# Sigmoid cross-attention: the last key's contribution moved from PE's output product to a POOL term that DVE's extraction starts from

## The reference, cut to what matters

```python
def _L1_xattn_ref(query, key, value, Wq, Wk, Wv, Wo):
    H, D, scale = 16, 16, 16 ** (-0.5)
    q = (query @ Wq.T).reshape(B, L, H, D) * scale
    k = (key @ Wk.T).reshape(B, -1, H, D)
    v = (value @ Wv.T).reshape(B, -1, H, D)
    scores = jax.nn.sigmoid(jnp.einsum('blhd,bshd->bhls', q, k))
    o = jnp.einsum('bhls,bshd->blhd', scores, v).reshape(B, L, E)
    return o @ Wo.T

x = x + _L1_xattn_ref(_layernorm(x, axis=-1), ctx_1024, ctx_1024, ...)   # x: [128, 32, 256], ctx_1024: [128, 257, 256]
```

## Time and profile before

| | |
|---|---|
| runs, us | 3064.57, 3067.11, 3067.53 |
| median of the runs, us | 3067.11 |
| the profiled execution's own time, us | 3058.71 |
| its span (first to last instruction), us | 3056.9 |
| mean clock granted to PE, of 2.4 GHz | 0.926 |
| PE busy over the span | 2633.2 us (86%), 31182 matmuls |
| DVE, ACT, POOL busy over the span | 66%, 59%, 54% |
| this layer | 1594 to 2294 us of the span |
| PE, DVE, ACT, POOL busy in these 700 us | 665, 509, 472 and 418 us |

### The profile page before, as it was taken

One profiled execution on the slowest core, in us unless ns is written; L12 is line 12 of the kernel. 1 busy time (PEld: TensorE's weight loads), 2 busy tenths in 40 slices (PEclk: granted clock), 3 DMA queues, 4 the chain that ended last, 5 costly groups with the idle time before them and its releaser, 6 DMA issues. The chain is left out here.

```text
span 3056.9 us, 81164 instructions
## 1 busy us (share of the span) xinstructions
PE 2633.2 (86%) x31182; PEld 2052.3 (67%) x31182; DVE 2019.7 (66%) x4510; ACT 1814.4 (59%) x4252; POOL 1652.4 (54%) x1589
## 2 busy tenths in 40 slices
PE   2999999999985988986797999999994888527998
PEld 2888888888863655553355888888873666416776
DVE  4677777777764777776346777777766888653443
ACT  2667767667666777772345777777763666343333
POOL 3666666666635777773006666666644777142332
PEclk9999999999996999887798999999996999558999
DMA  5333332223300000000002212221200000451110
GB/s 145 85 84 85 84 82 76 75 77 84 92 28 1 1 1 1 1 1 14 16 15 84 64 49 64 64 64 49 64 18 16 2 2 2 170 181 48 38 40 26
DMA packets 120951, 160.04 MB, mean 52 GB/s; under 512 B 11456, under 2 KB 107840, under 8 KB 118400
## 3 DMA queue, kind: packets, MB, share of 16 engines
q1 hardware_dynamic: 115904, 140.28, 16.1%
q0 software_dynamic: 4672, 14.57, 1.3%
HBM read 139.99 MB, written 14.83 MB: 51 GB/s over the span
## 5 line engine op out<-in xcount | busy, mean ns | idle before, releaser
L570 ACT ACTIVATE x_prob<-x_prob,x_nm 128x257 f32<-128x257 f32 x512 | 254.5, 499 | 212.7 <-DVE x_nm L656 212.7
L1894 DVE TENSOR_TENSOR_SCAN m_s<-m_a,m_psD 128x1024 f32<-128x1024 f32 x128 | 284.9, 2267 | 3.0 <-PE m_psD L1721 2.9
L656 DVE CUSTOM_DVE_ANT_0 x_prob<-x_psS,x_masked,x_lastv 128x256 f32<-128x256 f32 x512 | 217.3, 481 | 104.0 <-PE x_psS L476 100.7
L1195 DVE SCALAR_TENSOR_TENSOR x_pTl<-x_psS,x_pTh 128x1024 f16<-128x1024 f32 x128 | 156.7, 1225 | 144.9 <-ACT x_pTh L1103 144.9
L1833 ACT ACTIVATE m_a<-m_dt,m_rate 128x248 f32<-128x248 f32 x512 | 206.9, 493 | 0.0
L2778 ACT ACTIVATE e1t_g<-e1t_psH,e1t_bias 128x128 f32<-128x128 f32 x312 | 89.2, 368 | 171.1 <-PE e1t_psH L2727 171.1
L1605 POOL TENSOR_TENSOR m_s<-m_s 128x1024 f32<-128x1024 f32 x64 | 150.6, 2354 | 68.5 <-DVE m_s L1894 68.5
L883 POOL TENSOR_TENSOR x_qbdh<-x_qh,all_mask4h 128x1024 f16<-128x1024 f16 x32 | 60.6, 1894 | 215.8 <-DVE x_ql L1176 215.8
L1116 ACT ACTIVATE x_vh<-x_psV 128x512 f16<-128x512 f32 x128 | 76.4, 597 | 134.4 <-PE x_psV L922 134.4
L875 POOL TENSOR_TENSOR x_ctxl<-x_ctx,x_ctxh 128x512 f16<-128x512 f32 x128 | 149.7, 1170 | 10.7
L318 POOL TENSOR_TENSOR x_ctxl<-x_ctx,x_ctxh 128x512 f16<-128x512 f32 x128 | 148.3, 1159 | 10.7
(11 more groups left out here) (591 smaller groups left out, 10617.9 us busy)
## 6 DMA issues: line engine op xcount, KB each, us to landing
x_ctx<-in_ctxT SPq DMA_DIRECT2D x64, 1024.0 KB, 6.2
x_mraw<-in_mask SPq DMA_DIRECT2D x128, 128.5 KB, 6.0
x_vxr<-x_vx SPq DMA_DIRECT2D x32, 512.0 KB, 6.9
e1r_stage<-in_L_ffn_w SPq DMA_DIRECT2D x16, 1024.0 KB, 5.0
e_rows<-e1r_pad POOLq DMA_DIRECT2D x1, 5070.0 KB, 19.6
e1t_row<-e_rows SPq DMA_DIRECT2D x39, 130.0 KB, 2.1
all_xres<-in_x SPq DMA_DIRECT2D x1, 4096.0 KB, 14.4
x_vxr<-x_vx SPq DMA_DIRECT2D x128, 32.0 KB, 3.5
```

The lines of the kernel that those rows point to most:

```text
L570: last = act.activation(prob[b % NP][:, s, :], prob[b % NP][:, s, :], ACT.Exp, bias=nm[b % NP][:, s:s + 1], scale=-1.0, accum_out=sm[b // ...
L656: dve.tensor_tensor_reduce(prob[b % NP][:, s, 0:LAST], psS[:, s * LAST:(s + 1) * LAST], masked[g % 2][:, j, :], -SC, lastv[g % 2][:, j, s: ...
L1195: dve.scalar_tensor_tensor(pT[c % 4][1][:].rearrange("p r k n -> p (r k n)"), psS[c % 2][:], PS, pT[c % 4][0][:].rearrange("p r k n -> p ( ...
L1894: dve.tensor_tensor_scan(states, rates, psD[at % 2][:], 0.0, ALU.mult, ALU.add).then_inc(scan_done, 1)
```

## The change

The last key's term no longer goes through psO. `last_scores` multiplies by a 128x128 matrix `same_head` that is 1 where two channels belong to the same head, so that the score of a head comes out on each of its 16 channels, for both halves of the channels (two matmuls into 256 columns of psM instead of two that add up in 64 rows). ACT makes one sigmoid of it (128x256, f32). The last key's values are made with channels on partitions and kept in SBUF in f32 (`vx`). POOL's `last_term` multiplies the two into `term` (128x256, f32) in the place of `own_rows`. DVE's extraction makes all four passes, the first with `term` as what is added to; ACT's pass goes. The two matmuls at the end of `attend`, the f16 copies and low parts of the last probabilities, the writes to DRAM and the four row loads of each group go.

```diff
-        (vxp,) = parts("vx", [P, D], 1)
-        vxr = [sb(f"vxr{n}", [64, GB, D], F16) for n in range(2)]
-        vxm = [sb(f"vxm{n}", [64, GB, D], F16) for n in range(2)]
-        own_head, head_sum = sb("own_head", [64, D], F16), sb("head_sum", [P, C, 64], F32)
+        vx = sb("vx", [P, NT, C, GB], F32)
+        same_head = sb("same_head", [P, P], F32)
...
-        px32 = sb("px32", [64, P], F32)
-        px3 = [sb(f"px3_{n}", [64, P], F16) for n in range(2)]
+        px = [sb(f"px{n}", [P, C * P], F32) for n in range(2)]
+        term = [sb(f"term{n}", [P, C, GB, T], F32) for n in range(2)]
...
-        psA, psX = psM[:, 0:256], psM[0:64, 256:384]
+        psA, psX = psM[:, 0:256], psM[:, 256:512]
...
-            sync.dma_start(own_head[:], d["x1_own_head"]).then_inc(const_in, 16)
-            sync.dma_start(head_sum[:], d["x1_head_sum"]).then_inc(const_in, 16)
+            sync.dma_start(same_head[:], d["x1_same_head"]).then_inc(const_in, 16)
...
-            def load_vx(i, gp):
-                g = i * 2 + gp
-                wait_apart(sync, vxm_ready, g - 1, sync_passed)
-                for r in range(4):
-                    src = vx_dram[r % 2:r % 2 + 1, bass.ds(g * GB, GB), :].to_broadcast([16, GB, D])
-                    sync.dma_start(vxr[gp][16 * r:16 * r + 16], src).then_inc(vxr_in[gp], 16)
-
             load(0, 0)
             load(0, 1)
-            sync.wait_ge(vx_lo, 1)
-            for k in range(2):
-                sync.dma_start(vx_dram[k], vxp[k][:]).then_inc(vx_out, 16)
-            sync.wait_ge(vx_out, 32)
 
             def body(i):
                 for gp in range(2):
                     if not (isinstance(i, int) and i == 0):
                         load(i, gp)
-                    load_vx(i, gp)
...
-            def own_rows(i, gp):
+            def last_term(i, gp):
                 g = i * 2 + gp
-                wait_apart(pool, vxr_in[gp], (i + 1) * 64, pool_passed)
-                wait_apart(pool, pv_mm, (g - 1) * GB, pool_passed)
-                pool.tensor_tensor(vxm[gp][:], vxr[gp][:], own_head[:].unsqueeze(1).to_broadcast([64, GB, D]), ALU.mult)\
-                    .then_inc(vxm_ready, 1)
+                pool.wait_ge(px_sig, g + 1)
+                wait(pool, o_ext, 2 * (g - 1))
+                pool.tensor_tensor(term[gp][:].rearrange("p c j t -> p (c j) t"),
+                                   px[gp][:].rearrange("p (n t) -> p n t", t=T),
+                                   vx[:, g].rearrange("p c j -> p (c j)").unsqueeze(2).to_broadcast([P, C * GB, T]), ALU.mult)\
+                    .then_inc(term_done, 1)
...
                     if j == 3:
-                        own_rows(*after)
+                        last_term(*after)
...
-                products(psV[:, 0:D], [part(lastp, lambda x: x[:, cc, :]) for cc in range(C)],
-                         [part(W["v"], lambda w: w[:, cc, :]) for cc in range(C)]).then_inc(vx_mm, 1)
+                for h in range(C):
+                    last = products(psV[:, h * NB:(h + 1) * NB],
+                                    [part(W["v"], lambda w: w[:, cc, h * P:(h + 1) * P]) for cc in range(C)],
+                                    [part(lastp, lambda x: x[:, cc, :]) for cc in range(C)])
+                last.then_inc(vx_mm, 1)
...
-                    last = pe.matmul(psX, head_sum[:, c, :], qx[:, c, :], start=c == 0, stop=c == C - 1)
+                    last = pe.matmul(psX[:, c * P:(c + 1) * P], same_head[:], qx[:, c, :], start=True, stop=True)
...
-                if j == 0:
-                    pe.wait_ge(vxm_ready, i * 2 + (gp + 1))
-                    pe.wait_ge(px_lo, i * 2 + (gp + 1))
                 for kt in range(2):
                     for half in range(C):
                         to = (half * 2 + j % 2) * P
                         for v, p in ((0, 0), (0, 1), (1, 0)):
                             for r in range(RG):
-                                pe.matmul(psO[64 * r:64 * r + 64, to:to + P],
+                                last = pe.matmul(psO[64 * r:64 * r + 64, to:to + P],
                                           V[c % 4][v][:, kt, half * P + 64 * r:half * P + 64 * r + 64],
                                           pT[c % 4][p][:, r, kt, half * P:(half + 1) * P],
-                                          start=j % 2 == 0 and kt == 0 and half == 0 and (v, p) == (0, 0), stop=False,
+                                          start=j % 2 == 0 and kt == 0 and half == 0 and (v, p) == (0, 0),
+                                          stop=kt == 1 and (v, p) == (1, 0),
                                           skip_group_check=True)
-                for half in range(C):
-                    to = (half * 2 + j % 2) * P
-                    last = pe.matmul(heads(psO)[:, half * 2 + j % 2], vxm[gp][:, j, half * P:(half + 1) * P],
-                                     px3[gp][:, j * T:(j + 1) * T].unsqueeze(1).to_broadcast([64, 4, T]),
-                                     start=False, stop=True, skip_group_check=True)
...
-                wait(act, px_lo, g)
-                act.activation(px32[:], psX, ACT.Sigmoid, scale=SC).then_inc(px_sig, 1)
-                act.wait_ge(px_sig, g + 1)
-                wait(act, pv_mm, (g - 1) * GB)
-                act.activation(px3[gp][:], px32[:], ACT.Copy, scale=PS).then_inc(px_hi, 1)
+                wait(act, term_done, g - 1)
+                act.activation(px[gp][:], psX, ACT.Sigmoid, scale=SC).then_inc(px_sig, 1)
...
-            def extract(i, c):
-                gp, jp = c // 4, c % 4 // 2
-                act.wait_ge(pv_mm, i * 8 + c + 2)
-                act.activation(pair_of(oT[gp], jp), own_cols(0), ACT.Copy,
-                               scale=con["mask4"][:, 0:1]).then_inc(o_part, 1)
...
-            act.wait_ge(const_in, 48)
+            act.wait_ge(const_in, 32)
...
-            act.activation(vxp[0][:], psV[:, 0:D], ACT.Copy).then_inc(vx_hi, 1)
+            for h in range(C):
+                last = act.activation(vx[:, :, h, :], psV[:, h * NB:(h + 1) * NB].rearrange("p (g j) -> p g j", j=GB),
+                                      ACT.Copy, scale=PS)
+            last.then_inc(vx_done, 1)
...
-            def lo_px(i, gp):
-                g = i * 2 + gp
-                dve.wait_ge(px_hi, g + 1)
-                dve.scalar_tensor_tensor(px3[gp][32:64, :], px32[32:64, :], PS, px3[gp][32:64, :], ALU.mult, ALU.subtract)\
-                    .then_inc(px_lo, 1)
...
             def extract(i, c):
-                q = i * 4 + c // 2
+                q, g = i * 4 + c // 2, i * 2 + c // 4
                 gp, jp = c // 4, c % 4 // 2
                 dst = pair_of(oT[gp], jp)
-                for h in range(1, 4):
-                    dve.wait_ge(o_part, q * 3 + h)
-                    last = dve.scalar_tensor_tensor(dst, own_cols(h), con["mask4"][:, h:h + 1], dst,
-                                                    ALU.mult, ALU.add)
+                dve.wait_ge(pv_mm, i * 8 + c + 2)
+                dve.wait_ge(term_done, g + 1)
+                wait(dve, ob_hi, g - 1)
+                for h in range(4):
+                    if h > 0:
+                        dve.wait_ge(o_part, q * 3 + h)
+                    last = dve.scalar_tensor_tensor(dst, own_cols(h), con["mask4"][:, h:h + 1],
+                                                    dst if h > 0 else pair_of(term[gp], jp), ALU.mult, ALU.add)
                     last.then_inc(o_part if h < 3 else o_ext, 1)
```

More of the change, by code:

```diff
@@ L781, in sigmoid_attention @@
         pT = parts("pT", [P, RG, 2, C * P], 4)
-        px32 = sb("px32", [64, P], F32)
-        px3 = [sb(f"px3_{n}", [64, P], F16) for n in range(2)]
+        px = [sb(f"px{n}", [P, C * P], F32) for n in range(2)]
+        term = [sb(f"term{n}", [P, C, GB, T], F32) for n in range(2)]
         oT = [sb(f"oT{n}", [P, C, GB, T], F32) for n in range(2)]
         (obp,) = parts("ob", [P, C, P], 1)
-        vx_dram = nc.dram_tensor("x1_vx", (2, NB, D), F16, kind="Internal").ap()
         psK, psV, psO, psM = ps("psK", [P, 512]), ps("psV", [P, 512]), ps("psO", [P, 512]), ps("psM", [P, 512])
         psS = [ps(f"psS{n}", [P, RG * 512]) for n in range(2)]
-        psA, psX = psM[:, 0:256], psM[0:64, 256:384]
+        psA, psX = psM[:, 0:256], psM[:, 256:512]
         const_in, ctx_in = sem("const_in"), [sem(f"ctx_in{n}") for n in range(2)]
-        vx_out, vxr_in = sem("vx_out"), [sem(f"vxr_in{n}") for n in range(2)]
         pool_passed, sync_passed = sem("pool_passed"), sem("sync_passed")
-        last_hi, last_lo, kx_mm, kx_done, vx_mm, vx_hi, vx_lo = (sem(k) for k in (
-            "last_hi", "last_lo", "kx_mm", "kx_done", "vx_mm", "vx_hi", "vx_lo"))
-        ctx_hi, ctx_split, vxm_ready = sem("ctx_hi"), sem("ctx_split"), sem("vxm_ready")
+        last_hi, last_lo, kx_mm, kx_done, vx_mm, vx_done = (sem(k) for k in (
+            "last_hi", "last_lo", "kx_mm", "kx_done", "vx_mm", "vx_done"))
+        ctx_hi, ctx_split = sem("ctx_hi"), sem("ctx_split")
```

(14 more changed lines are left out.)

11 lines of the change are left out of this document (2 added, 9 removed).

## The result

The changed kernel takes 3037.68 us (median of 6 runs, 3030.02 to 3042.58), the kernel before, measured beside it, 3064.76 (6 runs, 3057.07 to 3067.53). The ratio is 0.9912, with an interval of 0.9892 to 0.9933: faster by 27 us, 0.9%. The forecast was 3038.2. The profiled execution took 3039.65 us (span 3037.9, mean clock 0.923).

A forecast was written before the change was run, and what follows sets the result against it. PE was taken to bound the kernel. Savings of 28.2 us (`attend`) and 0.7 (start), all else 0, made 28.9 off 3058.71, so 3029.8 profiled; with runs 8.4 above that, 3038.2 us, range 3033 to 3055.

The forecast's parts named there:

- What bounds the kernel: In the second cross-attention PE sets the slot; what leaves PE's row leaves the kernel until a feeding engine is late.
- The end of `attend`: On PE, dropping the two L1043 matmuls saves 0.22 us in each of 128 batches, 28.2 us.
- the 15.4 us bound: Lower bound of the saving at the end of `attend`, if leaving column tiles costs a second 0.10 us.
- the rival on a dearer change of shape: On PE, the shape change out of column tiles costs 0.10 us more: 3051.0 us, chance 0.05.
- The last key's scores: On PE, once a group, L961 with 128 columns takes 1.29 us against 1.30 before: 0 change.
- The rival of 3059: On PE, f32 weights of 128 columns load in twice the time of 64: 21 us lost, 3059, chance 0.04.
- The start: Two constant loads become one ahead of the context load, so PE's first `keys` starts earlier: 0.7 us.
- ACT and SP: ACT's lighter work and SP's 128 dropped row loads change nothing, as PE did not wait for them: 0.
- DVE's room: The longer extraction before `attend` makes PE wait only for what `ln` lasts beyond 0.89 us: 0.
- The rival on the psO wait: `attend` waits for DVE's extraction of psO, 0.47 us in 32 groups, 15.0 us: 3053.2, chance 0.15.
- The slower rival: `ln` on DVE is held by two POOL operations; PE waits 1.09 us a group, 34.9 us: 3073, chance 0.05.
- The sum: All terms together: 28.2 + 0 + 0.7 - 0 = 28.9 us saved.

The follow-up runs named there:

- two kernels: The kernel before with 128 weight columns instead of 64 in the last key's scores, 3063.00 us, and the changed kernel, 3037.68 us.
- the spare operations: Changed kernel plus an unread POOL multiplication behind the last key's term, of 510, 780 or 2880 elements: 3052.82, 3038.59 and 3059.36 us.
- `ln` at 1.23: Changed kernel plus an unread POOL multiplication of 510 elements behind the last key's term: 3052.82 us.
- the 2880 elements: Changed kernel plus an unread POOL multiplication of 2880 elements behind the last key's term: 3059.36 us, a group 0.69 us longer.

## Why the prediction was right, step by step

- **What bounds the kernel: right.** What left PE's row left the time: two matmuls out of the old kernel gave the whole gain.
- **The end of `attend`, 0.22 us a batch, 28.2 in all: right.** 0.37 became 0.15, and the groups' 0.87 x 32 is 27.9. The inference from the step out of row tiles to the step out of column tiles held, so the 15.4 us bound and the rival on a dearer change of shape are gone. The make-up (0.10 for the change, 0.053 a matmul) was tested with one matmul less: 0.06.
- **The last key's scores, 0: right, its side argument weak.** 1.29 was forecast and came. But the loads of 128 columns do take 192 ns and not 141; they cost nothing because they are hidden, not because width hardly matters. The rival of 3059 is gone by two kernels. It took more than the rule on columns for it: that the load is also paid for was my own addition.
- **The start, 0.7 us: right by the rows**, 0.70 and 0.81 in the two profiles. It is too small to be seen in the layer: the old kernel without L1043, with both constant loads and 9.58 us to the first `keys`, has a layer of 664.9 all the same.
- **ACT and SP, 0: right**, as the old kernel without L1043 keeps both at their old work and is as fast.
- **DVE's room: right, and it was the step to check.** The threshold of 0.89 for `ln` is 0.84 in the runs. `ln` was to be 0.4 to 0.5, or 0.8 if the next L873 (now L853) holds it: it is 816 ns, held by L853 (1895.12, with `ln` from 1895.07). That leaves 0.04 us. The new product was given 622 ns and takes 608. The margin is thin: for the spare operations my values of `ln` were off by 0.1 to 0.2, so that the wait came out at nothing here, and not at a tenth or two a group (3 to 6 us in all), was in part luck.
- **The rival on the psO wait was real, only not this kernel's phase.** With `ln` at 1.23 the group stalls by 0.39. The conditions under which I let it happen were wrong in one point: I wrote that only a POOL operation of 1.5 us or more brings the old phase back, but the phase also depends on the length of PE's slot (`ln` was 404 ns with one L1043 and 523 with none, and POOL unchanged).
- **The slower rival** (`ln` held long enough to pay back the gain) was followed to 0.69 a group. The point from which it decides, 0.90 a group, would be `ln` of some 1.74 us, an estimate from the line of the points above (0.84 + 0.90); it was not reached.
- **The sum, 28.9 us**, against 29.0 in the layer with the second profile of the changed kernel (26.5 with the first) and 27 in the medians. That the median came within 1 us of the forecast is partly luck: the profiled execution, forecast at 3029.8, took 3039.65, because the rest of the program was longer in it by 7.5 us and the layer, mostly for the clock at its start, by 2.5.

## What to carry to other kernels

When one engine never waits, price an edit by the distance between the starts of its records, change of array shape included, and then ask which wait comes nearest to the new, shorter slot. Here that wait had 0.04 us left, and what decided it was not the work of another engine but its phase: an operation that shares a resource with a neighbour should stand where a stretch of several tenths costs nothing. Count the changes of shape in a loop before its matmuls; moving two steps side by side brought a further 0.43 a group, half of the 0.87 that removing two matmuls had brought, with no work removed.

## What the runs showed of the hardware

- A DVE operation from SBUF to SBUF (L174, 128x256 f32) that has to wait for a POOL operation ends 0.14 to 0.15 us behind it, however long that is: it takes 404 ns when nothing holds it, and 3.46 us in the group of the 2880 elements, where POOL's 4.99 us from 1674.79 end at 1679.78 and `ln` at 1679.92. DVE's passes that read PSUM beside the same POOL operations kept their 0.34 to 0.35 us. The Trainium skill (SBUF — State Buffer, SBUF: two separate sides) calls the SBUF ports that DVE and POOL share an exclusive lock for the whole instruction of the one that comes first; the rows agree on the whole instruction. The start of a record is not yet the claim, though. In the changed kernel `ln` is recorded from 1895.07, L853 from 1895.12, and `ln` was the one that waited. In the old kernel with one L1043 it is further ahead, and there POOL waits: its L875 takes 1.27 us where 1.16 is usual, and `ln` takes 404 ns (DVE, then POOL):

```profile
1694.78 0.40 DVE L174 TENSOR_SCALAR x_xn<-all_xres,all_mean,all_rstd 128x256 f32<-128x256 f32 x1
...
1694.92 1.27 POOL L875 TENSOR_TENSOR x_ctxl<-x_ctx,x_ctxh 128x512 f16<-128x512 f32 x1
```

  So 0.05 us ahead is too little here and 0.14 is enough. A PE slot shorter by 0.06 us moved `ln` from the one side (1919.23 against 1919.28 in the kernel before) to the other, with nothing edited on DVE or POOL.
- A change of the array's shape costs 0.09 to 0.10 us on top of the matmul before it, in each pair of shapes that these traces have: full to column tiles, column tiles to full, row tiles to full, full to row tiles, row tiles to column tiles, column tiles to row tiles.
- The f32 weight loads of the last key's scores take 192 ns with 128 columns against 136 with 64, and these matmuls still start 0.11 apart; the loads of the f32 transposes take some 141 with 128 columns, and why these are shorter stays open.
